# A graph layer on one core: output of 88 blocks in two rounds inside the loop, the last ten blocks on four engines, and the last group's work ahead of older work

## The chip, the cores and the metric

The kernel runs on one core of one Trainium2 chip. The time is that of one execution on the device, in microseconds (us). Smaller is better. The engines are TensorE (PE), VectorE (DVE), ScalarE (ACT), GpSimd (POOL) and SyncE (SP). Each runs its own list of instructions in order, and they meet at semaphores. DMAs are issued by SyncE, ScalarE and GpSimd, each through a queue of its own.

## The reference

One layer of a graph network on 12,500 nodes with 128 features and 200,000 edges, in float32. Cut to what matters:

```
h = relu(layernorm(x))                      # 12500 x 128
skip = linear(h);  lin1 = linear(h)         # per node
weight = silu(silu(rbf(dist) @ fc_w1) @ fc_w2) @ fc_w3   # per edge
msg = product of weight, lin1[src] and edge_attr_4       # per edge, 256 wide
agg = segment_sum(msg, dst) / clip(count, 1)             # per node
out = x + skip + tanh(agg_s @ alpha_w * a) * linear2(agg)
# dst is sorted: dst = sort(int(12500 * u**2)), u uniform in [0, 1)
```

## The kernel before

**First stage (lines 257 to 625).** The 12,500 nodes are 98 blocks of 128. Layer norm and the first linear layer are computed four blocks at a time; GpSimd does the subtraction (L379), and `lin_table`, the result, goes to DRAM. Then VectorE places the groups of edges: for each it finds the first block of nodes that they touch (`blk_f`, `blk_i`).

**The edge loop.** `SLOTS = 4` groups of 768 edges are one iteration; `ITERS = 65` iterations are groups 0 to 259, and a short group 260 holds the last 320 edges. The group number is n = 4i + u. Per group:
- GpSimd gathers the source rows of `lin_table` (L939), six tiles of 128 edges with one indirect DMA each, into `lin_g`. In every third iteration one of the 24 tiles is fetched row by row by SyncE instead. The buffer of a group is free again once VectorE has read it four groups earlier.
- TensorE runs the three layers on the distances (`layer1` L967, `layer2` L977, `layer3` L987), with ScalarE's Silu between them.
- ScalarE scales gathered rows (L1112), VectorE forms the products and the message: `products` (L1324), `columns` (L1332 to L1343) and `late` (L1354 to L1364).
- TensorE sums the message within the group (`near_layer`, L999), ScalarE copies that (`copy_near`, L1120), TensorE takes it to the nodes of a block (`segment_sum`, L1011), ScalarE copies again (`copy_sums`, L1124), TensorE applies the second linear layer (`node_layer`, L1019 to L1021), and VectorE adds the result to `agg` (`accumulate`, two instructions at L1414).

The work is staggered: in the body of group n VectorE does `late` of n + 1 with `accumulate` of n - 1 inside, then `products` and `columns` of n + 2. `segment_sum` and `node_layer` use one bank, `ps_sums`, so each waits until the one before it has been read.

**Output inside the loop.** Since the edges are sorted by destination, blocks below a bound are final before the loop ends. One step is four blocks. In group 238, `early_scales` (VectorE, four instructions) and `early_tanh` (ScalarE) make the factors of the first 80 blocks, and `early_gains` follows in the next body. Then 20 steps run in groups 239 to 258, one per group: four ScalarE copies with a scale (`grow_early`, L1159), in the next group two VectorE additions with the skip term (`add_early`, L1386), and a 256 KB store from ScalarE's queue (`store_early`, L1166). The placement step checks that no late group touches those blocks; if one did, the number of passes over all edges would rise by one (L569 to L573).

**Closing block (L1484 on).** The 18 blocks that are left: five small VectorE instructions and a tanh make `gain`; then ScalarE copies three of each four blocks with their gain (L1548), VectorE adds them (L1536), does the other blocks alone (L1529), and SyncE stores (L1507, L1510).

## Time and profile before

| what | value |
|---|---|
| median of three runs | 2029.18 us (2028.21 to 2031.62) |
| the profiled execution, its own time | 2030.65 us |
| its span | 2028.9 us |
| mean granted TensorE clock | 0.922 of full speed |
| busy, share of the span: PE, DVE, ACT, POOL | 87%, 81%, 55%, 74% |
| VectorE idle before L619, first stage, released by a weight's DMA | 1.23 us |
| stores of the output inside the loop, issue to landing | 2.3 / 2.5 / 3.0 us (least, median, longest) |

The span is the part that the profiler records from the first to the last instruction; 1.75 us of the execution's own time lie around it. Busy time is the time in which an engine executes; register, branch, semaphore and DMA-issuing instructions do not count. An engine with less than 100% may still be the one that sets the pace, if each of its instructions is followed by a pause in which it prepares the next. In a timeline each row gives the start and the duration in us, the engine and line, the tiles, and in brackets how long the engine sat idle before it and what released it.

### The profile page before, as it was taken

The numbers are of one execution on the slowest core, as the hardware profiler recorded it, in microseconds if no ns is written. First come the engines' busy times: TensorE is split into PE (matmuls) and PEld (weight loads), VectorE is DVE, ScalarE is ACT, GpSimd is POOL, SyncE is SP. The second block draws the span as 40 slices with busy tenths as digits, with TensorE's granted clock in tenths as the row PEclk, the third lists the DMA queues.
The fourth block names the chain that finished last, engine by engine and source line by source line (L and its number), as shares of the span: only waits on it lengthen the run. The fifth ranks groups of instructions, "written<-read, shape, count | busy, mean of one in ns | idle before, by whom it ended". The sixth has DMA issues, their size and how long they took to land. (4 is left out here: it accounts for less than half of the span.)

```text
span 2028.9 us, 47569 instructions
## 1 busy us (share of the span) xinstructions
PE 1769.9 (87%) x9991; PEld 1204.0 (59%) x9991; DVE 1652.5 (81%) x4468; ACT 1116.4 (55%) x3263; POOL 1503.9 (74%) x1598
## 2 busy tenths in 40 slices
PE   6698889898899889879898898889889888988886
PEld 6465656665666666656565565556656555655654
DVE  8697878887888788878787778888777888888887
ACT  6565555565656556545455445455555555555665
POOL 6577777777777777777777777777777777777773
PEclk9698998998989899999899898998899899988988
DMA  8432332333233233222222222222222222222433
GB/s 241 101 72 67 66 72 62 71 70 71 63 71 70 62 71 72 56 61 61 60 58 60 61 60 58 61 60 57 60 61 61 57 61 60 58 60 63 93 93 83
DMA packets 329766, 143.35 MB, mean 71 GB/s; under 512 B 242627, under 2 KB 304380, under 8 KB 329580
## 3 DMA queue, kind: packets, MB, share of 16 engines
q0 software_dynamic: 49344, 101.13, 18.9%
q1 hardware_dynamic: 269676, 35.39, 11.4%
q10 hardware_dynamic: 10560, 5.24, 0.9%
q14 instruction: 178, 1.46, 0.2%
q8 instruction: 8, 0.13, 0.0%
HBM read 127.88 MB, written 13.75 MB: 70 GB/s over the span
## 5 line engine op out<-in xcount | busy, mean ns | idle before, releaser
L939 POOL DMA_INDIRECT lin_g<-lin_table,src_ix x1542 | 1467.8, 952 | 480.8 <-issue 471.9
L1112 ACT ACTIVATE lin_sh<-lin_g,harm 128x128 f32<-128x128 f32 x1563 | 483.5, 389 | 174.0 <-DMA lin_g<-lin_table,src_ix 116.8
L987 PE MATMUL ps_w<-w,h 128*128 128x256 f32 x1566 | 479.4, 450 | 4.8 <-DVE msg L1359 1.7
L999 PE MATMUL ps_near<-msg,onehot 128*64 128x257 f32 x3126 | 415.6, 402 | 0.0
L987 PEld LDWEIGHTS ps_w<-w,h 128*128 128x128 f32 x1566 | 369.3, 270 | 47.5 <-issue 10.4
L1324 DVE TENSOR_TENSOR lin_sh<-lin_g,ps_meta 128x576 f32<-128x576 f32 (+1 forms) x261 | 196.5, 753 | 232.4 <-DMA lin_g<-lin_table,src_ix 161.6
L1011 PE MATMUL ps_sums<-far_hot,near_sums 128*128 128x128 f32 x1044 | 202.2, 321 | 198.5 <-DVE agg L1414 195.3
L1011 PEld LDWEIGHTS ps_sums<-far_hot,near_sums 128*128 128x128 f32 x1044 | 152.0, 210 | 359.4 <-issue 350.8
L999 PEld LDWEIGHTS ps_near<-msg,onehot 128*64 128x64 f32 x3126 | 209.9, 143 | 174.2 <-issue 102.0
L1094 ACT ACTIVATE h<-ps_h 128x384 f32<-128x384 f32 x261 | 127.7, 489 | 235.9 <-PE ps_h L967 229.4
L967 PE MATMUL ps_h<-rbf,w 32*128 32x192 f32 x1044 | 240.2, 349 | 17.5 <-DVE rbf L1308 16.8
L1354 DVE TENSOR_TENSOR msg<-lin_sh,ps_w 128x576 f32<-128x576 f32 (+1 forms) x261 | 195.1, 747 | 53.5 <-PE ps_w L987 25.4
L977 PE MATMUL ps_h<-h,w 64*64 64x384 f32 x1044 | 226.4, 510 | 0.0
L1343 DVE TENSOR_REDUCE dot<-lin_sh 128x192 f32<-128x576 f32 (+1 forms) x261 | 210.2, 805 | 0.0
L1124 ACT ACTIVATE sumT<-ps_sums 128x256 f32<-128x256 f32 x261 | 99.7, 382 | 193.2 <-PE ps_sums L1011 166.3
L1120 ACT ACTIVATE near_sums<-ps_near 128x257 f32<-128x257 f32 x261 | 98.9, 379 | 193.6 <-PE ps_near L999 188.9
L1364 DVE TENSOR_TENSOR msg<-w_s,ps_meta 128x576 f32<-128x576 f32 (+1 forms) x261 | 194.2, 744 | 0.0
L967 PEld LDWEIGHTS ps_h<-rbf,w 32*128 32x128 f32 x1044 | 162.7, 185 | 37.1 <-issue 20.2
L1101 ACT ACTIVATE h<-ps_h 128x384 f32<-128x384 f32 x261 | 128.0, 491 | 74.8 <-PE ps_h L977 72.8
L1340 DVE TENSOR_TENSOR onehot<-iota,ps_meta 128x384 f32<-128x384 f32 (+1 forms) x261 | 142.6, 546 | 0.0
L1019 PEld LDWEIGHTS ps_sums<-near_sums,far_hot 128*128 128x128 f32 x522 | 77.6, 188 | 102.2 <-issue 100.9
L1414 DVE SCALAR_TENSOR_TENSOR agg<-ps_sums,at_lo,agg 128x130 f32 x261 | 91.1, 349 | 57.6 <-PE ps_sums L1021 56.2
(163 smaller groups left out, 1901.7 us busy)
## 6 DMA issues: line engine op xcount, KB each, us to landing
lin_g<-lin_table SPq DMA_DIRECT2D x2688, 0.5 KB
lin_g<-lin_table,src_ix POOLq DMA_INDIRECT x1542
dist_in<-in_edge_weight SPq DMA_DIRECT2D x67, 96.0 KB
xq<-in_x SPq DMA_DIRECT2D x24, 256.0 KB, 4.0
lin_table<-lin_out SPq DMA_DIRECT2D x24, 256.0 KB, 2.9
x_in<-in_x SPq DMA_DIRECT2D x24, 256.0 KB
harm<-in_edge_attr SPq DMA_DIRECT2D x66, 48.0 KB
out_dram<-x_in ACTq DMA_DIRECT2D x10, 256.0 KB, 2.5
```

The lines of the kernel that those rows point to most:

```text
L939: pool.indirect_dma_start(slot_tiles(s, u)[rows, t, :], None, lin_table, bass.IndirectOffsetOnAxis(ap=src_ix[rows, s.phase, u, col:col + 1 ...
L967: mm = pe.matmul(ps_h1[:, part * SEG:(part + 1) * SEG], w1[rows, 2 * k + part, :], rbf[rows, :], start=True, stop=True)
L977: mm = pe.matmul(ps_h2[lo:lo + HID, 0:UNIT], w2[lo:lo + HID, lo:lo + HID], h1[lo:lo + HID, k % 2, :], start=True, stop=True)
L987: mm = pe.matmul(ps_w[:, 2 * j * P:(2 * j + 2) * P], cols[:, j, :], w3[:], start=True, stop=True)
L999: mm = pe.matmul(ps_near[half * NEAR:(half + 1) * NEAR, 0:MSG + 1], onehot[:, u % 2, t, :], msg[:, u % 2, t, :], start=(j == 0), stop=(j = ...
L1011: mm = pe.matmul(ps_sumT[:, c * P:(c + 1) * P], near_sums[:, u % 2, c * P:(c + 1) * P], far_hot[:, u, :], start=True, stop=True)
L1112: last = act.activation(lin_sh0[:, u % 2, j, :], slot_tiles(s, u)[:, j, :], ACT.Copy, scale=harm[:, s.phase, u, harm_col(j):harm_col(j) + 1])
L1324: dve.tensor_tensor(lin_sh[:, h], lin_v(s, u)[:, h], sh_vec(u)[:, h], ALU.mult).then_inc(lin_sh_ready, 1)
L1340: dve.tensor_tensor(onehot[:, u % 2, h], iota1[:, 0:NEAR].unsqueeze(1).to_broadcast([P, TILES, NEAR])[:, h], ps_key(u).unsqueeze(2).to_bro ...
L1343: dve.tensor_reduce(dot[:, h], lin_sh[:, h].rearrange("p t m c -> p t c m"), AX_X, ALU.add).then_inc(dot_ready, 1)
L1354: dve.tensor_tensor(o10[:, h], scaled[:, h, MUL:].rearrange("p t (m c) -> p t m c", m=3), spread_m(w_part(2))[:, h], ALU.mult).then_inc(o1 ...
L1364: dve.tensor_tensor(o01[:, h], spread_m(w_s[:])[:, h], sh_vec(u)[:, h], ALU.mult).then_inc(msg_ready, 1)
```

## The change

1. The output inside the loop has 22 steps (88 blocks) for 20. They come in two rounds: `ROUNDS = ((0, 17, 222), (17, 22, 249))` gives the first step, the end, and the group in which the factors are made. Steps 0 to 16 run in groups 223 to 239, steps 17 to 21 in 250 to 254. The check in the placement step is done for both rounds.
2. In the last iteration the short group's `near_layer`, `copy_near` and `segment_sum` stand ahead of group 259's `segment_sum`, `copy_sums` and `node_layer`. Its sums use the bank `ps_h1`, so it doesn't wait for `ps_sums`. On VectorE, `accumulate` of 258 stands behind the whole message of 260.
3. The closing block has ten blocks. ScalarE copies seven of them with their gain; GpSimd adds three and then one, VectorE adds three and does three alone; SyncE issues three stores and ScalarE one.

```diff
-EARLY = 20
-SLOT0 = ITERS * SLOTS - 1 - EARLY
-LOOPED = ITERS - 8
-LATE0 = SLOT0 - 1
+ROUNDS = ((0, 17, 222), (17, 22, 249))
+EARLY = ROUNDS[-1][1]
+LATE0 = ROUNDS[0][2]
+LOOPED = ITERS - 11
 TAIL = NBLK - EARLY * NB
...
-                        dve.tensor_reduce(late_least[:], blk_f[:, LATE0:], AX_X, ALU.min).then_inc(turns_step, 1)
-                        dve.wait_ge(turns_step, 2)
-                        dve.tensor_scalar(missed[:], late_least[:], float(EARLY * NB - 1), None, ALU.is_lt).then_inc(turns_step, 1)
+                        for r, (_, _, late0) in enumerate(ROUNDS):
+                            dve.tensor_reduce(late_least[:, r:r + 1], blk_f[:, late0:], AX_X, ALU.min).then_inc(turns_step, 1)
                         dve.wait_ge(turns_step, 3)
-                        dve.tensor_tensor(passes_i[:], turns_all[:], missed[:], ALU.add).then_inc(place_step, 1)
+                        for r, (_, end, _) in enumerate(ROUNDS):
+                            dve.tensor_scalar(missed[:, r:r + 1], late_least[:, r:r + 1], float(end * NB - 1), None, ALU.is_lt).then_inc(turns_step, 1)
+                        dve.wait_ge(turns_step, 5)
+                        dve.tensor_tensor(missed_any[:], missed[:, 0:1], missed[:, 1:2], ALU.max).then_inc(turns_step, 1)
+                        dve.wait_ge(turns_step, 6)
+                        dve.tensor_tensor(passes_i[:], turns_all[:], missed_any[:], ALU.add).then_inc(place_step, 1)
...
+                            if not last_group(i):
+                                at_least(pe, sumT_ready, n)
+                                pe.wait_ge(agg_ready, n + 1)
...
+                            if not last_group(i):
+                                pe.wait_ge(agg_ready, n + 1)
...
+                                if last and u == SLOTS - 1:
+                                    near_layer(ITERS, 0)
                                 segment_sum(i, u)
                                 if share and u == 1:
                                     skip_layer(i)
@@ -1067,9 +1108,8 @@
                         with pe.Fori(STEPS + 1, ITERS - 1) as i:
                             body(i)
                         body(ITERS - 1, last=True)
+                        segment_sum(ITERS, 0)
                         node_layer(ITERS - 1, SLOTS - 1)
-                        near_layer(ITERS, 0)
-                        segment_sum(ITERS, 0)
                         node_layer(ITERS, 0)
...
+                                if last and u == SLOTS - 1:
+                                    copy_near(ITERS, 0)
                                 copy_sums(i, u)
...
+                                if scales_in(i, u) is not None:
+                                    early_tanh(scales_in(i, u))
...
-                        copy_near(ITERS, 0)
                         copy_sums(ITERS, 0)
...
-                                late(s, u + 1, sooner)
-                                if slot_is(i, u, SLOT0):
-                                    early_gains()
+                                if last and u == SLOTS - 1:
+                                    late(s, u + 1)
+                                    accumulate(*sooner)
+                                else:
+                                    late(s, u + 1, sooner)
+                                if scales_in(i, u - 1) is not None:
+                                    early_gains(scales_in(i, u - 1))
...
+            def add_grown(eng, blks, rows):
+
+                for part in range(2):
+                    done = eng.tensor_tensor(in_parts(result[rows, blks, :])[part], by_parts(grown[rows, blks, :])[part],
+                                             in_parts(result[rows, blks, :])[part], ALU.add)
+                return done
+
+            def step_blocks(n):
+                return slice(n * NB, n * NB + OWN)
...
-                    for n in range(LAST):
-                        sp.wait_ge(new_ready, n + 1)
-                        sp.dma_start(node_rows(out, EARLY + n), result[:, n * NB:(n + 1) * NB, :]).then_inc(out_stored, 16)
-                    sp.wait_ge(new_ready, LAST + 1)
-                    for r in range(REST):
-                        sp.dma_start(rest_rows(out, r), result[0:REST_ROWS[r], LAST * NB + r, :]).then_inc(out_stored, 16)
+                    sp.wait_ge(rest_ready, 1)
+                    sp.dma_start(rest_rows(out, 1), result[0:REST_ROWS[1], LAST * NB + 1, :]).then_inc(out_stored, 16)
+                    sp.wait_ge(own_ready, 1)
+                    sp.wait_ge(added_by_pool, 1)
+                    sp.dma_start(node_rows(out, EARLY), result[:, 0:NB, :]).then_inc(out_stored, 16)
+                    sp.wait_ge(added_by_dve, 1)
+                    sp.dma_start(node_rows(out, EARLY + 1), result[:, NB:2 * NB, :]).then_inc(out_stored, 16)
                     sp.wait_ge(out_stored, 16 * (LAST + REST))
 
...
-                    for n in range(LAST + 1):
-                        for j in range(BY_ACT if n < LAST else 0, blocks(EARLY + n)):
-                            blk, rows = n * NB + j, slice(0, P if n < LAST else REST_ROWS[j])
-                            for part in range(2):
-                                last = dve.scalar_tensor_tensor(out=in_parts(result[rows, blk, :])[part], in0=by_parts(whole[rows, blk, 1:COUNT])[part],
-                                                                scalar=gain[rows, blk:blk + 1], in1=in_parts(result[rows, blk, :])[part],
-                                                                op0=ALU.mult, op1=ALU.add)
-                        if n < LAST:
-                            rows = result[:, n * NB:n * NB + BY_ACT, :]
-                            dve.wait_ge(grown_ready, n + 1)
-                            for part in range(2):
-                                last = dve.tensor_tensor(in_parts(rows)[part], by_parts(grown[:, n % 2])[part], in_parts(rows)[part], ALU.add)
-                        last.then_inc(new_ready, 1)
+                    own_block(OWN, slice(0, P)).then_inc(own_ready, 1)
+                    own_block(LAST * NB + 1, slice(0, REST_ROWS[1])).then_inc(rest_ready, 1)
+                    own_block(NB + OWN, slice(0, P)).then_inc(own_ready, 1)
+                    dve.wait_ge(grown_ready, 2)
+                    add_grown(dve, step_blocks(1), slice(0, P)).then_inc(added_by_dve, 1)
 
                 @block.scalar
                 def _(act):
                     act.wait_ge(pre_ready, 1)
                     act.activation(alpha[:], pre[:], ACT.Tanh).then_inc(alpha_ready, 1)
                     act.wait_ge(gain_ready, 1)
-                    for n in range(LAST):
-                        at_least(act, new_ready, n - 1)
-                        for j in range(BY_ACT):
-                            blk = n * NB + j
-                            last = act.activation(grown[:, n % 2, j, :], whole[:, blk, 1:COUNT], ACT.Copy, scale=gain[:, blk:blk + 1])
+                    for blks in (range(0, OWN), range(NB, NB + OWN), range(LAST * NB, LAST * NB + 1)):
+                        for blk in blks:
+                            last = act.activation(grown[:, blk, :], whole[:, blk, 1:COUNT], ACT.Copy, scale=gain[:, blk:blk + 1])
                         last.then_inc(grown_ready, 1)
+                    act.wait_ge(added_by_pool, 2)
+                    act.dma_start(rest_rows(out, 0), result[0:REST_ROWS[0], LAST * NB, :]).then_inc(out_stored, 16)
+
+                @block.gpsimd
+                def _(pool):
+                    pool.wait_ge(grown_ready, 1)
+                    add_grown(pool, step_blocks(0), slice(0, P)).then_inc(added_by_pool, 1)
+                    pool.wait_ge(grown_ready, 3)
+                    add_grown(pool, slice(LAST * NB, LAST * NB + 1), slice(0, P)).then_inc(added_by_pool, 1)
```

TensorE at the end of the loop; near_sums and far_hot are the short group's or 259's inputs of `segment_sum`. Before:

```order
L1011 MATMUL ps_sums<-far_hot,near_sums 128x128 x2
L987 MATMUL ps_w<-w3,h2 128x256 x3
L999 MATMUL ps_near<-msg,onehot 64x257 x6
L1019 MATMUL ps_sums<-near_sums,far_hot 128x1
L1020 MATMUL ps_sums<-w_lin2,sumT 128x65
L1021 MATMUL ps_sums<-w_lin2,sumT 128x64
L1011 MATMUL ps_sums<-far_hot,near_sums 128x128 x2
L1019 MATMUL ps_sums<-near_sums,far_hot 128x1
L1020 MATMUL ps_sums<-w_lin2,sumT 128x65
L1021 MATMUL ps_sums<-w_lin2,sumT 128x64
L999 MATMUL ps_near<-msg,onehot 64x257 x3
L1011 MATMUL ps_sums<-far_hot,near_sums 128x128 x2
```

In the changed kernel, the same place, from group 259's near layer on:

```order
L1036 MATMUL ps_near<-msg,onehot 64x257 x6
L1058 MATMUL ps_sums<-near_sums,far_hot 128x1
L1059 MATMUL ps_sums<-w_lin2,sumT 128x65
L1060 MATMUL ps_sums<-w_lin2,sumT 128x64
L1036 MATMUL ps_near<-msg,onehot 64x257 x3
L1049 MATMUL ps_sums<-far_hot,near_sums 128x128 x2
L1049 MATMUL ps_h1<-far_hot,near_sums 128x128 x2
L1058 MATMUL ps_sums<-near_sums,far_hot 128x1
L1059 MATMUL ps_sums<-w_lin2,sumT 128x65
L1060 MATMUL ps_sums<-w_lin2,sumT 128x64
```

The short group's near layer (`64x257 x3`) has moved up by two steps, directly behind the node layer of group 258, and its `segment_sum` writes `ps_h1` directly behind that of group 259.

VectorE at the same place: the message of group 260, with the accumulation of 258 (L1414, later L1458) and the additions of an output step (L1386). Before:

```order
L1359 SCALAR_TENSOR_TENSOR msg<-dot,ps_w 128x3x32
L1405 TENSOR_LOAD blk_i
L1405 ISA x2
L1414 ISA
L1414 SCALAR_TENSOR_TENSOR agg<-ps_sums,at_lo,agg 128x130
L1414 ISA
L1414 SCALAR_TENSOR_TENSOR agg<-ps_sums,at_hi,agg 128x130
L1364 TENSOR_TENSOR msg<-w_s,ps_meta 128x3x3x32
L1386 TENSOR_TENSOR new_rows<-hT_in,skip 128x4x32
L1386 TENSOR_TENSOR new_rows<-hT_in,skip 128x4x3x32
```

In the changed kernel:

```order
L1401 SCALAR_TENSOR_TENSOR msg<-dot,ps_w 128x3x32
L1406 TENSOR_TENSOR msg<-w_s,ps_meta 128x3x3x32
L1449 TENSOR_LOAD blk_i
L1449 ISA x2
L1458 ISA
L1458 SCALAR_TENSOR_TENSOR agg<-ps_sums,at_lo,agg 128x130
L1458 ISA
L1458 SCALAR_TENSOR_TENSOR agg<-ps_sums,at_hi,agg 128x130
```

The last instruction of the message (L1364, later L1406) has moved ahead of the accumulation, and no output addition stands here any more.

## Rows read from the trace of the kernel before

**Rows 1.** Page, costliest groups: line, operation, tiles; busy, mean ns; idle before.
```profile
L939 POOL DMA_INDIRECT lin_g<-lin_table,src_ix x1542 | 1467.8, 952 | 480.8 <-issue 471.9
```

**Rows 2.** Timeline, GpSimd, 1700 to 1855 us: start, duration, line, tiles, idle.
```profile
1699.36 0.94 POOL L939 DMA_INDIRECT lin_g<-lin_table,src_ix  x1 [0.30 <-issue]
...
1854.26 0.94 POOL L939 DMA_INDIRECT lin_g<-lin_table,src_ix  x1 [0.30 <-issue]
```

**Rows 3.** Waits of VectorE, 1700 to 1860: total us, times, longest.
```profile
DVE lin_sh L1324 <- DMA lin_g<-lin_table,src_ix: 23.8, 18, 3.0
```

**Rows 4.** Timeline, VectorE, output additions: first and last beside gathers.
```profile
1873.59 0.90 DVE L1386 TENSOR_TENSOR x_in<-rows_in,skip 128x128 f32<-128x128 f32 x2
...
2000.57 0.90 DVE L1386 TENSOR_TENSOR new_rows<-hT_in,skip 128x128 f32<-128x128 f32 x2
```

**Rows 5.** Timeline, GpSimd, 1855 to 2006: the gathers over 1.0 us.
```profile
1874.23 1.08 POOL L939 DMA_INDIRECT lin_g<-lin_table,src_ix  x1 [0.30 <-issue]
...
1880.61 1.20 POOL L939 DMA_INDIRECT lin_g<-lin_table,src_ix  x1 [0.31 <-issue]
...
1909.61 1.25 POOL L939 DMA_INDIRECT lin_g<-lin_table,src_ix  x1 [0.30 <-issue]
...
1916.15 1.35 POOL L939 DMA_INDIRECT lin_g<-lin_table,src_ix  x1 [0.30 <-issue]
...
1924.06 1.55 POOL L939 DMA_INDIRECT lin_g<-lin_table,src_ix  x1 [0.30 <-issue]
...
1947.15 1.61 POOL L939 DMA_INDIRECT lin_g<-lin_table,src_ix  x1 [0.30 <-issue]
...
1955.31 1.45 POOL L939 DMA_INDIRECT lin_g<-lin_table,src_ix  x1 [0.30 <-issue]
...
1973.28 1.15 POOL L939 DMA_INDIRECT lin_g<-lin_table,src_ix  x1 [0.30 <-issue]
...
2000.97 1.31 POOL L939 DMA_INDIRECT lin_g<-lin_table,src_ix  x1 [0.30 <-issue]
```

**Rows 6.** Timeline, all engines, end of the loop.
```profile
2002.17 0.75 DVE L1324 TENSOR_TENSOR lin_sh<-lin_g,ps_meta 128x576 f32<-128x576 f32 x1 [0.56 <-DMA lin_g<-lin_table,src_ix]
...
2008.41 1.52 PE L999 MATMUL ps_near<-msg,onehot 128*64 128x257 f32 x12
...
2010.36 0.39 PE L1021 MATMUL ps_sums<-w_lin,sumT 128*128 128x64 f32 x2
...
2011.42 0.44 DVE L1364 TENSOR_TENSOR msg<-w_s,ps_meta 128x288 f32<-128x288 f32 x1
...
2013.62 1.51 PE L999 MATMUL ps_near<-msg,onehot 128*64 128x257 f32 x6
...
2017.29 0.39 PE L1021 MATMUL ps_sums<-w_lin,sumT 128*128 128x64 f32 x2
...
2018.09 0.34 DVE L1414 SCALAR_TENSOR_TENSOR agg<-ps_sums,at_hi,agg 128x130 f32 x1
```

**Rows 7.** Timeline, all engines, the closing block.
```profile
2020.57 0.18 DVE L1523 TENSOR_TENSOR gain<-alpha,scale 128x18 f32<-128x18 f32 x1 [0.28 <-ACT alpha L1542]
...
2020.79 3.81 ACT L1548 ACTIVATE grown<-agg,gain 128x128 f32<-128x128 f32 x12 [0.25 <-DVE gain L1523]
2021.81 0.73 DVE L1536 TENSOR_TENSOR skip<-grown,skip 128x96 f32<-128x96 f32 x2 [0.51 <-ACT grown L1548]
...
2025.58 0.92 DVE L1529 SCALAR_TENSOR_TENSOR skip<-agg,gain,skip 128x32 f32<-128x32 f32 x4
2026.52 0.82 SPq L1510 DMA_DIRECT2D out_dram<-skip  x2
```

**Rows 8.** Windows: each engine's busy us (count), clock, DMA share, GB/s.
```profile
2027.00:2028.00 1.00, 0.00 (x0) 0.00 (x0) 0.00 (x0) 0.00 (x0) 0.00 (x0) 0.50 0.93 262
```

**Rows 9.** Groups by shape: GpSimd's subtractions in the first stage.
```profile
L379 POOL TENSOR_TENSOR h<-xq,mean_all 128x512 f32<-128x512 f32 x24 | 25.8, 1073 | 18.0 <-DVE mean_all L497 13.8 <-PE psT L445 3.8
...
L379 POOL TENSOR_TENSOR h<-xq,mean_all 128x256 f32<-128x256 f32 x1 | 0.6, 612 | 1.4 <-PE psT L445 1.4
```

More of the change, by code:

```diff
@@ L93, with slot_of @@
 TURN = float(np.nextafter(np.float32(2 * np.pi), np.float32(0)))
+def slot_of(step):
+    for first, end, scales in ROUNDS:
+        if first <= step < end:
+            return scales + 1 + step - first
 @dataclass(frozen=True)
@@ L1413, in accumulate @@
                                 rows = agg[:, bass.ds(blk * COLS + k * COLS, COLS)]
-                                dve.scalar_tensor_tensor(out=rows, in0=ps_l2, scalar=part[:, bass.ds(g, 1)],
+                                dve.scalar_tensor_tensor(out=rows, in0=ps_l2(i), scalar=part[:, bass.ds(g, 1)],
                                                          in1=rows, op0=ALU.mult, op1=ALU.add).then_inc(added, 1)
@@ L1514, in _, with own_block @@
                 def _(dve):
+                    def own_block(blk, rows):
+                        for part in range(2):
+                            done = dve.scalar_tensor_tensor(out=in_parts(result[rows, blk, :])[part], in0=by_parts(whole[rows, blk, 1:COUNT])[part],
+                                                            scalar=gain[rows, blk:blk + 1], in1=in_parts(result[rows, blk, :])[part],
+                                                            op0=ALU.mult, op1=ALU.add)
+                        return done
                     dve.tensor_scalar(count[:], whole[:, :, COUNT], 1.0, None, ALU.max).then_inc(at_least_one, 1)
```

101 lines of the change are left out of this document (59 added, 42 removed).

## The prediction

> **What bounds the kernel now.** I read the page's table of groups first, to find what runs without a pause. The reader is to see that the gathers on GpSimd do: 1542 of 952 ns, with 480.8 us of idle time put down to "issue", which is 0.3 us behind each [rows 1]. Undisturbed, one takes 0.94 us and the next starts 1.249 us after it (125 starts from 1699.36 to 1854.26, 154.9 us in 124 steps [rows 2]), and 1542 x 1.249 = 1926 of the 2028.9 us. Next the waits of VectorE in that quiet stretch before any output step: 23.8 us in 18 waits for the rows that a gather brings [rows 3]. So VectorE, busy as it is, follows the gathers, and the other engines follow it. Work that is added to VectorE, ScalarE or TensorE inside the loop is free so long as it neither holds up a gather nor leaves a lag at the end. Third, the timeline of the gathers beside VectorE's output additions (L1386) [rows 4, 5], to see whether such work does hold up a gather. Fourth, the timeline of the last slots, where the gathers have ended and the chain through TensorE decides [rows 6], and last that of the closing block, with the transfers [rows 7, 8].
>
> I call a group of 768 edges a slot, number 4i + u; 259 is the last full one, 260 the short one. G is the end of the closing block's gain (2020.57 + 0.18 = 2020.75).
>
> **Start of the kernel.** Three more tiny VectorE instructions in the placement step, each like its neighbours there (0.14 to 0.16 us), two more waits: 0.3 to 0.6 us. Shortly behind them VectorE sits idle for 1.23 us for a weight's DMA (the small table of the profile has it), which they cannot delay, so I take 0. Without that cover it would be 0.5. The test that they compute decides whether the loop runs a second time; see the last rival.
>
> **Output steps inside the loop.** Before, 20 steps ran in slots 239 to 258; now 17 run in 223 to 239 and 5 in 250 to 254. A step is four ScalarE copies, two VectorE additions (0.9 us together) and a 256 KB store from ScalarE's queue; the second round adds five small instructions on 20 columns and a tanh. VectorE's waits for rows, 1.3 us each on the mean in the quiet stretch, cover it in time. TensorE's program there is unchanged. Slots 255 to 259 lose their steps; that matters only in the end chain, below.
>
> What isn't covered is the hold on GpSimd. 18 pairs of additions ran while gathers were still being issued, from 1873.59 to 2000.57 [rows 4], and the nine gathers of [rows 5] that last over 1.0 us all start inside, or within 0.1 us of, such a pair. Over the usual 0.94 us they are late by 0.14, 0.26, 0.31, 0.41, 0.61, 0.67, 0.51, 0.21 and 0.37, in sum 3.49 us. The last fell in slot 260's gather, behind the rows that the end chain hangs on, so 3.12 counted. Gathers are the bound, so each hold is paid in full. The additions stand still relative to the gathers by their place in a cycle of twelve slots (three iterations, after which the pattern of gathers repeats). By slot modulo 12, in which the pair runs: place 0 held 0.14 and 0, place 1 0.26 and 0.21, places 2 to 4 nothing both times, 5 0.31 and 0.37, 6 0.41, 7 0.61, 8 and 9 nothing, 10 0.67, 11 0.51. Places seen twice agree to 0.14, so I trust the table for the new slots. Pairs now run in 224 to 240 and in 251 to 255:
> - 224 to 227 (places 8 to 11): 1.18
> - 228 to 239 (one full cycle): 0.07 + 0.24 + 0.34 + 0.41 + 0.61 + 0.67 + 0.51 = 2.85
> - 240: 0.07
> - 251 to 255 (11, 0, 1, 2, 3): 0.51 + 0.07 + 0.24 = 0.82
>
> Together 4.9 against 3.1: the loop gets **1.8 us longer**. Bounds: nothing, if the holds fall out as few as before, and 22 x 0.67 - 3.1 = 11.6 if every pair hits at the worst.
>
> The Trainium skill ("SBUF — State Buffer", section "Who interferes with whom") says that a VectorE instruction with two SBUF inputs contends with a GpSimd instruction that reads SBUF, but also infers that descriptor generation isn't stalled by a tensor_tensor. The gathers of [rows 5] agree with the first sentence, a gather reads its indices, and speak against the second. By the second the holds would have another cause, and the sum would be 1.8 us better.
>
> **The end of the loop.** Up to slot 258's node layer TensorE's order is the same and nothing in it waits for what is removed: it is bound from VectorE's work on slot 259 on, whose rows landed at 2002.17, and then runs without a gap from the near layer at 2008.41 to the end of the node layer at 2010.36 + 0.39 = 2010.75 [rows 6]. Then it waited for the accumulation on VectorE, did slot 259's products and node layer, and only at 2013.62 slot 260's near layer. Now that layer stands right there. Its message must be ready: VectorE loses one addition pair ahead of it (0.8 us) and the accumulation inside it with its wait (0.9), so the message ends near 2010.15 in place of 2011.42 + 0.44 = 2011.86. TensorE is the later: near layer 2010.75 to 2012.25 (1.51); slot 259's product to 2012.9, during which ScalarE copies 260's near sums (0.39); slot 260's product, in its own bank, to 2013.6; 259's node layer to 2014.5, while ScalarE copies both sums; 260's node layer to 2015.4 (0.9, as this layer took before 2010.75); its accumulation on VectorE, which then ended 0.75 behind the layer (2017.29 + 0.39 = 2017.68 to 2018.09 + 0.34 = 2018.43): **2016.1**. Against 2018.43 a gain of **2.3 us**. Bounds 1.5 (near layer only at 2011.5, if the message is later) and 2.8.
>
> **Closing block.** From 2018.43 to G nothing changes but 10 columns for 18 in five small instructions: 0.05. Before, 8.15 us from G to the span's end. Now, counted from G: ScalarE's copies take 3.81 / 12 = 0.32 each; three are ready at 1.05, six at 2.0, seven at 2.3. VectorE's own three blocks are done at 1.3 (four of its instructions took 0.92 [rows 7]) and its additions run from 2.0 to 2.75 (0.73). GpSimd's additions aren't in the trace. The nearest rows are its subtractions, 1.07 us for 512 elements and 0.61 for 256 [rows 9]: 0.15 + 1.8 ns per element, so 0.32 + 0.67 = 1.0 for 96 and 288, and 0.53 for the block alone. They run from 1.05 to 2.1 and from 2.3 to 2.85. For the clash with VectorE's instructions on the same tiles I add 0.2 to each. So the first 256 KB go at 2.3, the second at 2.95 to 3.33, ScalarE's 64 KB at 3.1 or a little later. Before, the end came 1.56 us after the end of the last issue, of 42 KB (2026.52 + 0.82 to 2028.9) [rows 7]; 214 KB more at the 262 GB/s of 2027 to 2028 [rows 8] are 0.8, and 0.2 for what the 64 KB take of it: 3.33 + 1.56 + 0.8 + 0.2 = 5.9. A gain of **2.25 us**. Bounds: 2.8 without clash and sharing, 1.0 if GpSimd takes twice as long on these strided tiles.
>
> The same page says that in such a clash the later instruction waits for the whole of the earlier one. By that the two engines' additions would go strictly one after the other and the second 256 KB would leave at 3.3 at the latest, 0.4 of gain less. No row of before has both engines at such tiles.
>
> **Sum.** -2.3 - 2.25 - 0.05 + 1.8 = -2.8 us. The profiled execution took 2030.65 (span 2028.9 and 1.75 around it), which gives 2027.85; the median shown is 1.47 lower, 2029.18, and so the forecast is **2026.4**. Under 0.2% (4.06 us) is about what a measurement of this kernel can't tell from no change, and this stays under it.
>
> **Rivals.**
> - The holds don't grow (another cause, or luckier places): -2.3 - 2.25 - 0.05 = -4.6, 2024.6, just faster. For it: four of the twelve places rest on one sighting each. Against: places seen twice repeat, and there are 22 pairs for 18.
> - GpSimd is slow in the closing block: its first additions take 2 us and the second 1, so its output leaves at 4.3 and the gain there is 1.0: -1.55 in all, 2027.6. For it: it is the one engine whose work there no row shows. Against: its subtractions ran beside a busy VectorE.
> - Slower: the holds at every place. The pairs in the first round shift the pattern, so that nearly each pair meets a starting gather. From a mean hold of 0.53 (11.7 us in 22) the change loses more than it gains with 0.2% on top, 0.35 is break-even; at the worst, 0.67, 14.7 - 3.1 - 4.6 = +7, 2036.2. For it: 0.66 to 0.67 did happen. Against: the mean was 0.19.
> - The test on late groups fails and all 65 iterations run twice, about 1950 us more. By the reference's destinations (12500 u squared, sorted), group 222 starts in block 70 where 68 is enough and group 249 in block 89 where 88 is. Practically excluded.
>
> **Chances.** Forecast 0.64, first rival 0.20, second 0.10, third 0.05, last 0.01. Faster by over 0.2%: most of the first rival and the fast edge of the forecast, 0.25. Slower: the third, the last, and a little for an unseen lag, 0.08. The rest, 0.67, within 0.2%. Range: from 2023.9 (all gains at their bounds, -5.3) to 2028.6 (-0.6: the second rival with holds 1 us above the table).
>
> **What would show it.** Gathers over 1.0 us beside output additions: eleven to thirteen, late by 4.9 us in sum, and the last gather starting some 1.8 us later than 2003.82. From the landing of slot 259's rows (VectorE's L1324) to the loop's last accumulation 13.9 us in place of 16.3. From G to the end 5.9, with GpSimd's four additions in 1.5. It is wrong if the last gather starts no later, if slot 260's near layer waits for its message, or if GpSimd's additions end after VectorE's.

## The result and the profile after

Over 21 runs of each, the changed kernel took 2025.11 us in the median (2021.53 to 2027.54), the kernel before 2028.36 (2026.41 to 2032.16). The ratio is 0.9981, 95% interval 0.9975 to 0.9987: **3.9 us faster, between 2.6 and 5.1** (the two medians lie 3.25 apart). The forecast was 2.8.

The profiled execution of the changed kernel took 2024.00 us, its span 2022.1. Its parts, beside those of before, all read from timelines:

| part | before | after |
|---|---|---|
| start of the span to the first gather | 67.11 | 65.44 |
| first gather to the start of the last | 1936.71 | 1935.47 |
| last gather to the end of the last accumulation | 14.61 | 12.55 |
| from there to the gain, G | 2.32 | 2.22 |
| G to the end of the span | 8.15 | 6.42 |

The first row can't be put down to the change: over this and eleven further profiles of this study the first gather starts between 64.4 and 66.6 us with (but for the three small instructions) the same first stage, and the span difference of 6.8 us overstates the change by it. The second row holds two effects that both vary from one execution to the next: gathers held beside the output additions (3.4 us before, 3.7 after) and gathers held beside the 24 skip additions of the loop's first 25 iterations, which the change leaves alone (5.3 before, 3.9 after, and 3.7 to 6.1 in eight profiles with the same additions). So it became 1.2 us shorter by a part that isn't the change's. The third and the last are the change's own.

**The gathers** still run without a pause [rows 1]; the page's group (line, operation, tiles, count; busy us, mean ns; idle before):

```profile
L976 POOL DMA_INDIRECT lin_g<-lin_table,src_ix x1542 | 1466.5, 951 | 480.9 <-issue 469.3
```

**The holds** answer to [rows 4, 5]. A gather is called late by what the distance from its start to the next start exceeds the usual 1.249 us. Timeline of GpSimd, the first three long gathers (start, duration), and of VectorE, the additions that they start in (L1430):

```profile
1758.50 1.30 POOL L976 DMA_INDIRECT lin_g<-lin_table,src_ix  x1 [0.30 <-issue]
...
1765.09 1.27 POOL L976 DMA_INDIRECT lin_g<-lin_table,src_ix  x1 [0.30 <-issue]
...
1772.90 1.46 POOL L976 DMA_INDIRECT lin_g<-lin_table,src_ix  x1 [0.30 <-issue]
```

```profile
1758.09 0.89 DVE L1430 TENSOR_TENSOR new_rows<-hT_in,skip 128x128 f32<-128x128 f32 x2
...
1764.47 0.91 DVE L1430 TENSOR_TENSOR x_in<-rows_in,skip 128x128 f32<-128x128 f32 x2
...
1772.65 0.88 DVE L1430 TENSOR_TENSOR new_rows<-hT_in,skip 128x128 f32<-128x128 f32 x2
```

These three start 0.25 to 0.62 us behind the start of a pair, when 0.63 to 0.29 us of it are left, and are late by 0.51 to 0.32 us: about what is left of the pair. Nine are late by over 0.1 us (they start 0.10 to 0.65 us into a pair), in sum 3.7 us with the small ones. Not every gather that starts inside a pair is late: the one at 1789.67 starts 0.15 us into a pair and takes 0.96 us, the one at 1952.77 starts 0.10 into one and takes 1.62. In the profiles of the changed kernel and of the runs below that keep these additions, those that start 0.25 us or more behind the pair's start, with over 0.2 us of it left, are late in every case; of those that start sooner some are and some aren't, and why isn't shown.

**The end of the loop** answers to [rows 6]; timeline of all engines:

```profile
1999.72 0.76 DVE L1366 TENSOR_TENSOR lin_sh<-lin_g,ps_meta 128x576 f32<-128x576 f32 x1 [1.52 <-DMA lin_g<-lin_table,src_ix]
...
2005.96 1.52 PE L1036 MATMUL ps_near<-msg,onehot 128*64 128x257 f32 x12
...
2007.15 0.45 DVE L1406 TENSOR_TENSOR msg<-w_s,ps_meta 128x288 f32<-128x288 f32 x1
...
2007.90 0.39 PE L1060 MATMUL ps_sums<-w_lin,sumT 128*128 128x64 f32 x2
...
2008.22 1.51 PE L1036 MATMUL ps_near<-msg,onehot 128*64 128x257 f32 x6
...
2009.77 0.39 ACT L1160 ACTIVATE near_sums<-ps_near 128x257 f32<-128x257 f32 x1 [1.86 <-PE ps_near L1036]
...
2010.21 0.71 PE L1049 MATMUL ps_h<-far_hot,near_sums 128*128 128x128 f32 x4
...
2012.02 0.39 PE L1060 MATMUL ps_h<-w_lin,sumT 128*128 128x64 f32 x2
...
2013.11 0.35 DVE L1458 SCALAR_TENSOR_TENSOR agg<-ps_h,at_hi,agg 128x130 f32 x1
```

VectorE's L1366 at 1999.72 is the first work on slot 259's rows, and is released by their landing. TensorE goes from 259's near layer (2005.96) through 258's node layer (to 2008.29, an end that is modelled) straight into the short group's near layer at 2008.22. Its message had been ready since 2007.60. The two products follow, the second into `ps_h1` at 2010.21, and the last accumulation ends at 2013.46.

**The closing block** answers to [rows 7]; G is 2015.51 + 0.17 = 2015.68:

```profile
2015.51 0.17 DVE L1591 TENSOR_TENSOR gain<-alpha,scale 128x10 f32<-128x10 f32 x1 [0.28 <-ACT alpha L1602]
2015.72 2.15 ACT L1606 ACTIVATE grown<-agg,gain 128x128 f32<-128x128 f32 x7 [0.24 <-DVE gain L1591]
2015.72 1.35 DVE L1578 SCALAR_TENSOR_TENSOR skip<-agg,gain,skip 128x32 f32<-128x32 f32 x6
...
2016.79 2.28 POOL L1555 TENSOR_TENSOR skip<-grown,skip 128x96 f32<-128x96 f32 x4 [14.95 <-ACT grown L1606]
2017.61 1.18 DVE L1555 TENSOR_TENSOR skip<-grown,skip 128x96 f32<-128x96 f32 x2 [0.54 <-ACT grown L1606]
2018.24 0.41 SPq L1569 DMA_DIRECT2D out_dram<-skip  x1
2018.81 0.39 SPq L1571 DMA_DIRECT2D out_dram<-skip  x1
2019.10 0.36 ACTq L1609 DMA_DIRECT2D out_dram<-skip  x1
```

and the groups of line 1555, GpSimd's and VectorE's additions (count: least, median, longest ns; shapes):

```profile
L1555 POOL TENSOR_TENSOR skip<-grown,skip x4: 266/628/874, 2016.8 to 2018.3; 128x96 f32<-128x96 f32 x2, 128x288 f32<-128x288 f32 x1, 128x32 f32<-128x32 f32 x1
L1555 DVE TENSOR_TENSOR skip<-grown,skip x2: 595/626/656, 2017.6 to 2018.2; 128x96 f32<-128x96 f32 x1, 128x288 f32<-128x288 f32 x1
```

GpSimd needs 2.28 us for its four additions: 0.53 and 0.87 for the first two (of 96 and 288 elements, 1.37 together), 0.27 and 0.73 for the last block's (32 and 96). VectorE's shorter one, of 96 elements, lasts 0.66 us, where the same took 0.26 alone before. The first 256 KB are issued at G + 2.56, the second at 3.13, ScalarE's at 3.42. For the 2 us from G + 3.5 on the transfers run without a pause (view by windows: us, busy us of PE, PEld, DVE, ACT, POOL with counts, granted clock, DMA share, GB/s):

```profile
2019.18:2021.18 2.00, 0.00 (x0) 0.00 (x0) 0.00 (x0) 0.00 (x0) 0.00 (x0) 0.50 0.99 283
```

### The profile page after: what moved, and what is told of

It is laid out like the page before. It is cut to its first block and busy times, and to the rows that moved or that the text cites. A ratio compares the mean times of both kernels' runs of the same rounds, so it can differ in the third digit from the quotient of the medians.

```text
span 2022.1 us, 47507 instructions
## 1 busy us (share of the span) xinstructions
PE 1774.5 (88%) x9991; PEld 1204.1 (60%) x9991; DVE 1652.9 (82%) x4468; ACT 1115.9 (55%) x3267; POOL 1504.9 (74%) x1602
## 5 line engine op out<-in xcount | busy, mean ns | idle before, releaser
L1036 PE MATMUL ps_near<-msg,onehot 128*64 128x257 f32 x3126 | 424.3, 408 | 0.0
L1366 DVE TENSOR_TENSOR lin_sh<-lin_g,ps_meta 128x576 f32<-128x576 f32 (+1 forms) x261 | 196.5, 753 | 218.5 <-DMA lin_g<-lin_table,src_ix 140.1
L1036 PEld LDWEIGHTS ps_near<-msg,onehot 128*64 128x64 f32 x3126 | 214.2, 146 | 178.9 <-issue 109.9
L1406 DVE TENSOR_TENSOR msg<-w_s,ps_meta 128x576 f32<-128x576 f32 (+1 forms) x261 | 194.2, 744 | 0.0
L1458 DVE SCALAR_TENSOR_TENSOR agg<-ps_sums,at_lo,agg 128x130 f32 x260 | 90.7, 349 | 65.2 <-PE ps_sums L1060 63.1
```

The costliest lines, as they stand in the source:

```text
L1036: mm = pe.matmul(ps_near[half * NEAR:(half + 1) * NEAR, 0:MSG + 1], onehot[:, u % 2, t, :], msg[:, u % 2, t, :], start=(j == 0), stop=(j = ...
L1366: dve.tensor_tensor(lin_sh[:, h], lin_v(s, u)[:, h], sh_vec(u)[:, h], ALU.mult).then_inc(lin_sh_ready, 1)
L1406: dve.tensor_tensor(o01[:, h], spread_m(w_s[:])[:, h], sh_vec(u)[:, h], ALU.mult).then_inc(msg_ready, 1)
```

## The experiments

Each kernel was timed beside the kernel before, on the same chip. "Late gathers" below is the sum over the gathers that start inside an output addition. Waits, places and parts are read from one profiled execution of each kernel.

**1. Output additions with one operand from PSUM.** The changed kernel, with

```diff
-            early_grown = (rows_in[:], hT_in[:].rearrange("p (b c) -> p b c", c=DIM))
+            early_grown = (ps_skip[:].rearrange("p (b c) -> p b c", c=DIM),) * 2
...
-                            at_least(act, early_new_ready, n - 1)
+                            at_least(act, early_new_ready, n)
```

> The changed kernel, but ScalarE writes its four scaled blocks of an output step to PSUM (the bank ps_skip, free by then), so the 22 VectorE addition pairs read one operand from SBUF in place of two. Theory: an addition with two SBUF operands holds back a gather that starts inside it. Then the holds beside the 22 pairs (3.8 us in the changed kernel's profile) fall to under 0.3, the pitch of the gathers there is 1.25 us throughout, and the kernel is about 3.5 us faster than the changed one: ratio to the kernel before 0.9964. Rival one, the 256 KB stores or other traffic of a step hold the gathers: holds stay at 3 to 4 us, ratio 0.998. Rival two, any VectorE work at that place does: the same.

Measured: 2021.98 us against 2028.82, ratio 0.9966 (0.9953 to 0.9979). All 22 pairs run, as long as before, and no gather that starts in one is late. Timelines of VectorE and GpSimd, the pair that stands where the changed kernel's third long gather was:

```profile
1772.38 0.88 DVE L1430 TENSOR_TENSOR new_rows<-ps_skip,skip 128x128 f32<-128x128 f32 x2
```

```profile
1772.72 0.95 POOL L976 DMA_INDIRECT lin_g<-lin_table,src_ix  x1 [0.30 <-issue]
```

The gather starts 0.34 us into the pair and takes its usual 0.95 us. The length of the addition and the stores are the same. What has changed is the place of one operand, which ScalarE writes and VectorE reads, and one wait of ScalarE. That VectorE's reading is what counts, and not ScalarE's writing, is shown by run 6, where ScalarE's work is unchanged. So the hold comes from the two SBUF operands.

**2. The skip additions from PSUM too.** As run 1, and

```diff
-                            at_least(pe, sc_scaled, i)
+                            at_least(pe, skip_ready, i)
...
-                                last = act.activation(rows_in[0:rows, b, :], ps_skip[0:rows, b * P:(b + 1) * P], ACT.Copy,
+                                last = act.activation(ps_skip[0:rows, b * P:(b + 1) * P], ps_skip[0:rows, b * P:(b + 1) * P], ACT.Copy,
...
-                                last = dve.tensor_tensor(skip[:, bass.ds(skip_block(i, 0) * DIM, NB * DIM)], rows_in[:].rearrange("p b d -> p (b d)"),
+                                last = dve.tensor_tensor(skip[:, bass.ds(skip_block(i, 0) * DIM, NB * DIM)], ps_skip[:],
```

(and the same for the two blocks of the first iteration).

> As the run before, and the 24 skip additions of the first 25 iterations also read one operand from PSUM (ScalarE scales in place in ps_skip; TensorE's next transposes wait for the addition). Theory: of the 11 to 12 us by which gathers are late over the whole loop, the 7 before the output steps are those additions too; all but 1 to 2 us go, and the kernel is 8 to 10 us faster than the changed one: ratio to before about 0.993. No store runs beside these additions, so the rival of the stores expects nothing from this half: ratio 0.998, or slower if TensorE's new wait costs something.

Measured: 2015.71 us, ratio **0.9939** (0.9926 to 0.9951), and in a second session 0.9943. From the first gather to the last are 1927.83 us, 7.6 fewer than in the changed kernel. Of the fifteen gathers that still last over 1.05 us, thirteen start at one instruction, the only other one in the loop, apart from small ones for the factors, with two SBUF tensors and no PSUM; timelines of GpSimd and VectorE:

```profile
913.79 1.12 POOL L976 DMA_INDIRECT lin_g<-lin_table,src_ix  x1 [0.30 <-issue]
```

```profile
913.75 0.34 DVE L1337 TENSOR_TENSOR frac<-far,turn_half 128x192 f32<-128x192 f32 x1
```

It lasts 0.34 us, and the gather is 0.18 late. The thirteen make 2.3 of the 3.8 us of lateness that are left. The rest, a pause of 0.32 and many small ones, wasn't looked into. Beside the 24 skip additions two gathers are late, by 0.10 and 0.04 us, in place of 3.9 us.

**3. The new order alone**, on the kernel before: the changes to `near_layer`, `segment_sum`, `node_layer`, `copy_near`, `accumulate` and the bank (part 2 of the change), nothing else.

> The kernel before with the last group's new order alone (near layer, copy and sums of the short group ahead; its own bank; accumulation of 258 behind the message). Theory: the gain at the end of the loop is the order's. From the landing of slot 259's rows to the last accumulation 16.3 us become 14.0 to 14.8 (one output addition still stands ahead of the message), and the time falls by 1.6 to 2.4: ratio 0.9990. Rival: it came from the slots without output steps, then 16 us remain and the ratio is 1.0.

Measured: 2026.38 us, ratio 0.9988 (0.9980 to 0.9997). From VectorE's first work on 259's rows to the last accumulation 14.70 us. As the theory had it.

**4. The old order with the rest of the change**: all of part 2 of the change undone, of which this is TensorE's order.

```diff
-                                if last and u == SLOTS - 1:
-                                    near_layer(ITERS, 0)
                                 segment_sum(i, u)
...
-                        segment_sum(ITERS, 0)
                         node_layer(ITERS - 1, SLOTS - 1)
+                        near_layer(ITERS, 0)
+                        segment_sum(ITERS, 0)
```

> The changed kernel with the old order of the last group: two rounds and the new closing block alone. Theory: the end of the loop is back at 15.5 to 16.3 us from landing to last accumulation, the closing block stays at 6.4 us from gain to end in place of 8.15, the holds stay at 3.8 in place of 3.1: 1.2 us faster than before, ratio 0.9994. Rival (the closing block on four engines is worth all of it): ratio 0.998.

Measured: 2028.42 us, ratio 0.9999 (0.9990 to 1.0008). From landing to the last accumulation 16.25 us, from G to the end 6.50, late gathers 1.96 us. The interval holds the expected 0.9994 and shuts the rival's 0.998 out. Rounds and closing block without the order give no gain that can be measured, though the profile has the closing block's; the order alone gives 1.2 thousandths of the 1.9 (run 3, between 0.3 and 2.0).

**5. The closing block as it was, on ten blocks.** The changed kernel with lines 1484 on of the kernel before (`BY_ACT = 3`, no GpSimd).

> The changed kernel with the closing block written as before (ScalarE three of four blocks, VectorE the additions and the others, SyncE all stores), on the ten blocks that are left. Theory A: the gain in the closing block (8.15 to 6.4 us from the gain to the end) is that of eight blocks less, not of four engines: by the durations of before VectorE is done at 3.6 us, the stores are issued by 4.4, the end is at 6.0 to 6.4, and the time is that of the changed kernel, ratio 0.998. Theory B: GpSimd and the store from ScalarE's queue bring it: the end is at 7.0 or later and the kernel 0.6 us or more slower than the changed one.

Measured: 2023.87 us, ratio 0.9976 (0.9967 to 0.9986), no worse than with four engines. From G (2020.08 + 0.17 = 2020.25) to the end of the span at 2026.3 are 6.05 us, the lower end of theory A. Its timeline:

```profile
2020.08 0.17 DVE L1571 TENSOR_TENSOR gain<-alpha,scale 128x10 f32<-128x10 f32 x1 [0.28 <-ACT alpha L1590]
...
2021.30 0.72 DVE L1584 TENSOR_TENSOR skip<-grown,skip 128x96 f32<-128x96 f32 x2 [0.50 <-ACT grown L1596]
...
2022.05 1.42 SPq L1555 DMA_DIRECT2D out_dram<-skip  x2
...
2022.99 0.91 DVE L1577 SCALAR_TENSOR_TENSOR skip<-agg,gain,skip 128x32 f32<-128x32 f32 x4
2023.93 0.82 SPq L1558 DMA_DIRECT2D out_dram<-skip  x2
```

The first 256 KB leave at G + 1.80 in place of 2.56. The four engines cost 0.37 us here rather than bringing any; the eight blocks less bring 2.1. By the times the two closing blocks can't be told apart; from G to the end it is 6.05 and 6.09 us in the two profiles with the old one (this and run 10), and 6.41 to 6.50 in all eight with the new one.

**6. Additions twice.** The changed kernel with each pair done first into a spare tensor:

```diff
+                            for part in range(2):
+                                dve.tensor_tensor(in_parts(spare[:])[part], by_parts(early_grown[n % 2])[part],
+                                                  in_parts(skip_of[:, n * NB:(n + 1) * NB, :])[part], ALU.add)
```

> The changed kernel with each pair of output additions done twice, first into a spare tensor and then into the one that is stored. If VectorE instructions with two SBUF operands hold the gathers, the holds beside the output steps rise to about double, 4 to 9 us (3.8 in the changed kernel's profile, which two other profiles of like kernels put at 2.1 and 1.6 for theirs), one hold lasting up to 1.5 us no more than each of the four instructions allows, and the time by 2 to 5 us. If the holds come from anything else of a step they stay at 2 to 4 and the time stays.

Measured: 2034.10 us, ratio 1.0025 (1.0017 to 1.0034), so 9 us slower than the changed kernel. All lateness behind the first pair sums to 15.6 us, where the changed kernel has 3.9. Not double but four times: a gather that starts early in the first pair waits for the rest of both, as here, timelines of VectorE and GpSimd:

```profile
1829.44 0.88 DVE L1431 TENSOR_TENSOR spare<-rows_in,skip 128x128 f32<-128x128 f32 x2
1830.23 0.88 DVE L1434 TENSOR_TENSOR x_in<-rows_in,skip 128x128 f32<-128x128 f32 x2
```

```profile
1829.76 2.34 POOL L977 DMA_INDIRECT lin_g<-lin_table,src_ix  x1 [0.30 <-issue]
```

1.35 us of the two pairs are left when it starts, and it is 1.4 us late, through four additions. It is the gathers that last longer; the pauses between them add less than 0.5 of the 12.2 us by which the stretch from the first gather to the last has grown, so the added work of VectorE isn't what delays them. The direction was as expected, the size was underestimated by half.

**7. No stores in the loop** (and no wait for them behind it).

```diff
-                            act.dma_start(node_rows(out, n), early_new[n % 2]).then_inc(early_stored[n % 2], 16)
...
-                            at_least(dve, early_stored[n % 2], 16 * (n // 2))
```

> The changed kernel without the 22 stores inside the loop, so 88 blocks of the output are not written; all else stands. If the two SBUF operands hold the gathers: holds stay at 2 to 4 us and the time is that of the changed kernel, ratio 0.998. If the stores do: holds under 0.5 and 3 us faster.

Measured: 2024.68 us, ratio 0.9981 (0.9972 to 0.9990), late gathers 3.6 us. The stores have no part in it.

**8. VectorE's part of the closing block from PSUM**, on the kernel of run 2: ScalarE writes those three blocks to `grown_ps`, and

```diff
-                    add_grown(dve, step_blocks(1), slice(0, P)).then_inc(added_by_dve, 1)
+                    add_grown(dve, step_blocks(1), slice(0, P), grown_ps[:, 0:OWN, :]).then_inc(added_by_dve, 1)
```

> The kernel that takes both kinds of additions from PSUM, and in the closing block the three blocks that VectorE adds are written by ScalarE to PSUM too, so VectorE and GpSimd no longer both read two SBUF operands there. In the changed kernel VectorE's addition of 96 elements lasted 0.66 us in place of the 0.26 of before, beside GpSimd. Theory: it is back at about 0.3, the second store is issued 0.4 us sooner, and from the gain to the end 6.4 become 6.0 us; ratio to before about 0.9935. Rival: GpSimd's own speed sets it, and 6.4 stays.

Measured: 2016.59 us, ratio 0.9941 (0.9928 to 0.9954). The groups of both engines' additions:

```profile
L1557 POOL TENSOR_TENSOR skip<-grown,skip x4: 245/470/872, 2008.3 to 2009.9; 128x96 f32<-128x96 f32 x2, 128x288 f32<-128x288 f32 x1, 128x32 f32<-128x32 f32 x1
L1557 DVE TENSOR_TENSOR skip<-grown_ps,skip x2: 258/396/535, 2009.1 to 2009.3; 128x96 f32<-128x96 f32 x1, 128x288 f32<-128x288 f32 x1
```

VectorE's is back at 0.26 us and GpSimd's four take 1.95 in place of 2.28, so the two did get in each other's way. But that was GpSimd's last addition (0.41 us, 0.73 before); its first two take 0.53 and 0.87 us as in the changed kernel. So the first 256 KB still leave at G + 2.56, and G to the end is 6.47 us although the second leave 0.1 and ScalarE's 64 KB 0.3 us sooner. The transfers are as full as before in the 2 us from G + 3.5 on:

```profile
2010.73:2012.73 2.00, 0.00 (x0) 0.00 (x0) 0.00 (x0) 0.00 (x0) 0.00 (x0) 0.50 0.99 282
```

The rival was right: GpSimd's own share of the first step sets it.

**9. Additions from PSUM with the old closing block**, twice, and run 2 once more beside it. In the first session this kernel took 3180.75 us and the kernel before 3170.22, this one at a mean granted clock of 0.77 (ratio 1.0035, 1.0002 to 1.0069). There the gathers don't set the pace, they wait for VectorE (1072 us in 147 waits), and the additions from PSUM bring nothing. From G to the end it has 5.99 us. Why both took so long wasn't looked into.

> The kernel that takes both kinds of additions from PSUM, with the closing block written as before the change (no GpSimd in it). By the runs so far the old way ends 6.05 us after the gain on ten blocks, the four engines 6.4, because the first 256 KB leave at 1.8 in place of 2.55 us after the gain. Theory: 6.0 to 6.1 here too, and holds of the gathers as before in that kernel (2 to 3.5 us in the whole loop, at L1337's subtraction with two SBUF operands). Time 2015.3 us, ratio to before 0.9937, not separable from the kernel with four engines by the time, only by the profile. Rival: the difference came from where the loop ended, then 6.4 again.

> The same kernel as in the run before, where both it and the kernel before took 3170 us at a mean granted clock of 0.77 and nothing could be told. Additions from PSUM, old closing block. Theory: from the gain to the end 6.05 us, holds 2 to 3.5 us in the whole loop, ratio to before 0.9937. Rival: 6.4 us at the end, ratio 0.994.

> The kernel with both kinds of additions from PSUM and the closing block of four engines once more, beside the same with the old closing block, so that the two are compared on one chip. Theory: 0.3 to 0.4 us slower than the other, 6.4 us from the gain to the end; ratio to before 0.994. If the four engines are the better, it is the faster one.

Measured in the second session: 2019.05 us with the old closing block, ratio 0.9945 (0.9932 to 0.9959); 2020.11 with four engines, 0.9943 (0.9930 to 0.9957); before 2031.78. From G to the end 6.09 and 6.42 us, as expected; by the times the two are the same. All three kernels with both kinds of additions from PSUM beat both the kernel before and the changed one by more than their intervals.

## Why the prediction was right in its range and low in its size

**What bounds the kernel: right.** The gathers set the pace of the loop. Against the changed kernel, runs 1, 2 and 6 move the stretch from the first gather to the last by -2.9, -7.6 and +12.2 us, and the time follows, by about -3, -8.5 and +9 (by the ratios).

**End of the loop, -2.3 us: right**, step by step. From the landing of 259's rows to the last accumulation 13.74 us, foretold 13.9, before 16.26. TensorE was the later one, as said: the message was ready 7.9 us behind the landing, the near layer started 8.5 behind it. Run 3 shows the order alone at 1.2 thousandths. That the gain isn't the clock's is shown by runs 4 and 11: in both the granted clock is 1.00 in every 4 us window from 12 us before the last gather to 12 us behind it, and from 259's first work to the last accumulation it is 16.25 us in the old order and 13.73 in the new one. Other executions of the new order took longer at a lower clock (last section), so 2.3 is its gain in the good case.

**Closing block, -2.25 us: mis-sized.** It measured 8.15 - 6.42 = 1.73. The step that failed is GpSimd's additions: foretold 1.5 us plus 0.4 for the clash, measured 2.28, so the first 256 KB left at 2.56 in place of 2.3, the second at 3.13 in place of 2.95, and the 64 KB behind them at 3.42. The 0.4 for the clash, which no row of before could give, came near (1.95 to 2.28), but it isn't what cost time: the first two additions, which release the first store, take 1.37 us with and without the clash, against 1.0 foretold and 0.2 on top. A second step was off too. The prediction counted the end from the issue of the second store (3.33 + 2.56 = 5.9). That issue ended at G + 3.52, 0.19 later, and the end came 2.90 us behind it; that issue isn't what sets the end. In run 8 it came sooner and the end did not; in run 5 the first 256 KB left 0.76 us sooner, the last issue ended at G + 4.50, and the end came 0.37 us sooner. And the whole 1.73 comes from the eight blocks less; the spreading over four engines took 0.37 of it away (run 5). The clash itself, that VectorE's and GpSimd's additions hold each other up, is shown by run 8: it agrees with the sentence of the Trainium skill ("SBUF — State Buffer", section "Who interferes with whom") on two SBUF inputs.

**Holds, +1.8 us: the mechanism right, the size wrong.** Foretold were eleven to thirteen gathers of over 1.0 us, late by 4.9 us in sum; it was nine, late by 3.7 (over 0.1 us each). The step that failed is "the additions stand still relative to the gathers by their place in a cycle of twelve slots". Late gathers beside the output additions, pair by pair in us, in three executions with the pairs at the same 22 places:

| kernel | pairs 1 to 17 | 18 to 22 | sum |
|---|---|---|---|
| changed | 0, 0.35, 0.32, 0.51, 0, 0, 0.47, 0, 0, 0.16, 0, 0, 0, 0.13, 0.58, 0.52, 0 | 0.68, 0, 0, 0, 0 | 3.7 |
| run 4 | 0, 0.23, 0, 0.06, 0, 0.17, 0, 0, 0, 0.05, 0, 0, 0, 0, 0.56, 0.46, 0 | 0.06, 0, 0.37, 0, 0 | 2.0 |
| run 5 | 0, 0.14, 0.46, 0.43, 0, 0, 0, 0, 0, 0, 0.68, 0.45, 0, 0.19, 0.37, 0.46, 0 | 0.07, 0, 0.27, 0, 0 | 3.5 |

Places repeat in part, not enough to carry a sum, and the kernel with 20 pairs of run 3 had 1.6 where the one before had 3.4 with the same pairs. Two sightings in one execution that agreed were taken for a rule. Over six executions (these three, before, runs 3 and 7) the mean is 0.14 us per pair; four more of them ahead of the last gather are 0.6 us, not 1.8. Worked out again after the result, with 0.6 for the holds and 1.73 for the closing block the sum is -2.3 - 1.73 - 0.1 + 0.6 = -3.5, inside the measured interval. The two terms missed in opposite directions, the holds by 1.2 and the closing block by 0.5 us, and so cancelled in part; that is luck.

**The signs of being wrong.** The last gather was to start 1.8 us later, and the prediction called itself wrong if it started no later. It started 2.9 us sooner (2000.91 against 2003.82). 1.7 of that is the start of the first gather. The other 1.2 comes from the skip additions, which the change leaves alone: 1.4 us less were lost beside them, and 0.3 more beside the output additions. So the sign was a poor one: it looks at one execution, and what varies there is as large as the term. Slot 260's near layer did not wait for its message. GpSimd's additions did end after VectorE's (its last runs from 2018.34 to 2019.07, VectorE's end at 2018.79), but by the prediction's own sum, 3.1 against 2.75, they had to; that sign contradicts it. The lower end of its range, -5.3, isn't what its bounds add up to either (-2.8 - 2.8 - 0.05 = -5.65 with no holds).

The first rival (holds don't grow, -4.6) was nearer than its chance said: 0.7 us off, the forecast 1.1. Of the two reasons that it named, another cause is shut out: the additions are the cause. The other, luckier places, is part of what happened. The inference of the Trainium skill (the same page and section) that descriptor generation isn't stalled by a tensor_tensor does not carry over to these gathers (run 1 against the changed kernel, run 6). Whether it is their descriptor generation that waits or their reading of the indices, no run here parts.

**Not measured apart:** the placement step's three instructions. The first gather's start varies by 2 us among kernels with the same first stage, so 0.5 us couldn't be seen.

## What to carry to other kernels

Where GpSimd issues indirect gathers without a pause and they are the bound, look at every VectorE instruction that reads both operands from SBUF: a gather that starts inside one can lose what is left of it. Let the producer write one operand to a free PSUM bank; here that brought 8 to 9 us more (0.9939 against 0.9981), over twice what the change itself brought. Where the gathers weren't the bound (run 9, first session), it brought nothing. And don't spread the last block over a slow engine if the first large store waits for it: what matters is when the first transfer leaves.

## What the runs showed of the hardware

- A gather that starts inside a pair of VectorE additions of two SBUF operands, 0.25 us or more behind its start, is late by about what is left of the pair: up to 0.68 us for a pair of 0.9 us, and 1.4 us for two pairs in a row. With one operand in PSUM: 0 in 22 pairs in run 1, one of 22 late by 0.06 us in run 11. A gather that was issued before the pair starts isn't late (0.94 us).
- GpSimd's additions of 96, 288, 32 and 96 elements on 128 partitions took 1.95 us together beside additions of VectorE that read one SBUF operand (run 8), and 2.27 to 2.28 beside such as read two (seven profiles). The difference is in the last, 0.41 against 0.73 us; VectorE's addition of 96 elements took 0.26 against 0.66.
- The end of the loop varies with TensorE's granted clock shortly before it. From the last gather's start to the last accumulation the new order took 12.5 to 12.6 us in four profiles (the changed kernel, runs 2, 10 and 11) and 12.9 in a fifth (run 8), but 14.2 in run 1. Windows of 4 us of run 1, two ahead of the last gather at 1997.94 (PE, PEld, DVE, ACT, POOL busy us and counts; granted clock; DMA share; GB/s), and the same two of the changed kernel, ahead of 2000.91:

```profile
1985.90:1989.90 4.00, 0.61 (x3) 0.64 (x4) 3.97 (x11) 1.18 (x4) 3.08 (x4) 0.61 0.21 61
1989.90:1993.90 4.00, 4.00 (x15) 2.71 (x16) 3.64 (x10) 2.13 (x7) 3.09 (x4) 0.54 0.18 52
```

```profile
1988.90:1992.90 4.00, 2.50 (x11) 1.94 (x9) 3.12 (x10) 1.55 (x6) 3.08 (x4) 0.79 0.23 60
1992.90:1996.90 4.00, 4.00 (x23) 2.39 (x23) 3.74 (x11) 1.63 (x6) 3.07 (x4) 0.79 0.20 51
```

In run 1 TensorE was busy for 0.61 of the first 4 us, and the clock stood mostly at the lower of its two levels, 1.2 GHz, in both windows; in the changed kernel it was busy for 2.50 and the clock was at 2.4 GHz for somewhat over half of the time. In runs 3, 5, 6 and 7, where this part took 13.4 to 14.5 us, a 4 us window within 12 us before the last gather or 8 us behind it is at 0.50 to 0.57 as well. Busy time alone doesn't tell when the clock falls: in run 4 TensorE was busy for 2.47 of 4 us at the same place, and the clock was 1.00. The kernel before was at 0.78 and 0.80 at this place, like the changed one at 0.78 and 0.79, so the two profiles compare like with like. The clock is a likely reason why single executions of one kernel differ by 2 us and more. It was seen in the profiles, and not tried by itself.
